# Cross-attention and an FP4 feed-forward on one core: the up half goes by ScalarE and GpSimd, and the sequence is set anew

## The chip, the cores and the metric

The kernel runs on one core of a Trainium2 chip. The metric is the device time of one execution in microseconds. Five engines work side by side, each through its own instructions in order: TensorE (PE; its weight loads are PEld), VectorE (DVE), ScalarE (ACT), GpSimd (POOL) and SyncE (SP), which here issues all DMA transfers. Matmul results lie in PSUM, which GpSimd does not read in this kernel; everything that GpSimd works on is first brought to SBUF by ScalarE.

## The reference

`x` is (16, 512, 256), the context (16, 1601, 192), all float32. One batch element is one "batch" below.

```python
x = x + xattn(layernorm(x), ctx_768)        # 16 heads of 16; softmax(Q K^T / 4) V, then Wo and bias
x = x + ffn(layernorm(x))

def fp4_linear(x, w):                       # blocks of 16 along the last dim, scale = max|x| / 6
    xq = fp4_quant_dequant(x); wq = fp4_quant_dequant(w)
    return jnp.einsum('bsk,nk->bsn', xq, wq)
gate = fp4_linear(x, w_gate)                # 256 -> 704
y = fp4_linear(x, w_up)                     # 256 -> 704
h = jax.nn.silu(gate) * y
return fp4_linear(h, w_down)                # 704 -> 256
```

## The kernel before

**Bodies.** After a prologue ("start") the kernel runs 16 bodies, one a batch ("first", 14 "middle", "last"), and a "tail". A body does the attention of its own batch, the projections of the next batch, and the feed-forward of the batch before; so the feed-forward stands in 15 bodies and once in the tail. 512 query rows are four quarters of 128 rows.

**Steps.** A body has 52 steps: four groups of four heads, 13 key tiles of 128 keys (the last of 65). A step has four score matmuls (128 keys by 512 queries, line 1001), four exponentials on ScalarE (line 1140), and four "weighted" matmuls into `out_ps` (line 1014, fp32). The shift of the softmax is found ahead: for each group ahead of its turn 64 "pieces" (line 1027, 402 keys each) are multiplied, two at a time, and VectorE takes the maximum of each (line 1369). `PIECES_AT` says how many pairs of pieces a step has, `EARLY_PIECES` how many pairs are done in the prologue already.

**The sequence.** `sequence(kind)` writes down one order of all work, and TensorE, ScalarE and VectorE each follow it. Inside a step the order comes from a string of `STEP_ORDERS`: `S01` and `S23` are two scores each, `P` a share of the step's pieces, `V` the weighted matmuls of the oldest step not yet done, and `W` the side events due by half-step 2 x step + 1. Before, there are 13 strings, one for each key tile, used alike by the four groups. Side events ("rounds" where TensorE has work in them) are placed by half-steps: `POST_AT` for the feed-forward of the four quarters, `PRE_AT` and `OWN_AT` for the projections, `TAIL_AT` for the tail. The 17 entries of a quarter are heads_T, out_proj, ln2_stats, ln2_apply, xq_max, xq_scale, xq_T, three gate_up, h_max, h_small, h_scale, h_grid, two h_T, down. GpSimd and SP go by the events alone, in the order of their half-steps. All of these numbers stand in the file by hand; nothing is planned while the kernel runs.

**PSUM.** A ring of seven banks (`RINGS`) serves scores, pieces and rounds in the order of the sequence. `claim` makes TensorE wait until the bank's last user was released: a score by its exponential, a piece by its maximum, a round by whichever engine reads it last (`drained`). VectorE handles a round after the next piece or at the next round.

**A gate_up round.** For 256 hidden columns (the third has 192) TensorE fills one bank with gate (`work[:, 0:w]`) and up (`work[:, w:2w]`), six matmuls (line 964). Then:

```python
act.activation(tanh_g[...], work[:, 0:w], ACT.Tanh, scale=0.5)                       # L1118
dve.scalar_tensor_tensor(out=tanh_g[...], in0=tanh_g[...], scalar=1.0, in1=work[:, 0:w], ...)  # L1323
dve.scalar_tensor_tensor(out=q.h[...], in0=tanh_g[...], scalar=0.5, in1=work[:, w:2*w], ...)   # L1326
```

The last one releases the bank. `tanh_g` has two halves, used in turn; ScalarE waits by `silu_step` for the first product of the round before. Later `h_max`, `h_small` (VectorE), `h_scale` (GpSimd, lines 1428 and 1431) and `h_grid` with the rounding (VectorE lines 1201 and 1203, GpSimd from line 1418) make FP4 of `h`, `h_T` turns it, `down` multiplies it; ScalarE copies that result to `down_out` (line 1107) and GpSimd adds it to `x1` (line 1471). In the tail VectorE instead of GpSimd does the scaling, and the rounding of the quarters in `VECTOR_ROUNDS` (lines 1191 to 1195).

**Keys and queries.** `q_proj` and `k_proj` rounds are copied twice by ScalarE (1083, 1084), GpSimd subtracts to get the low part (1462), and SP's "stack" events then move both parts into `k_stack` and `q_stack`, which pieces and scores read.

Of the kernel before, what the change touches and what calls it, by code (L numbers as in the profile page):

```python
# [31 lines left out]
P = 128  # L32
# [33 lines left out]
]  # L66
TAIL_AT = [
# [7 lines left out]
OWN_AT = [6, 15, 15, 16, 18]  # L75
PRE_AT = [24, 27, 27, 30, 45, 45, 50, 56, 61, 61, 63, 66, 69, 69, 70, 71, 71, 72, 74, 76, 85, 99]
# [3 lines left out]
LN1 = 8  # L80

HEADS_OUT_AT = 3
MAX_AT = [22, 23]
PIECES_AT = [
# [4 lines left out]
]  # L89
EARLY_PIECES = 3  # L90
STEP_ORDERS = ['P S01 W P S23 P V', 'S01 P W P S23 P V', 'S01 P W S23 P V', 'S01 P W P S23 P V', 'S01 P W P S23 P V', 'S01 P W P S23 P V', 'S01 P W P S23 P V', 'S01 P W P S23 P V', 'S01 P W P S23 P V', 'S01 P W S23 P V', 'S01 P W P S23 P V', 'S01 P P S23 W P V', 'S01 P S23 P V']
# [8 lines left out]
VECTOR_ROUNDS = [1, 3]  # L100
# [92 lines left out]
def build(nc, x, ctx_768, Wq, Wk, Wv, Wo, bo, w_gate, w_up, w_down, out):  # L193
# [74 lines left out]
    for step in range(STEPS):  # L268
        ready = step - (STEPS - VALUES_LEFT)
        VALUES_LEFT -= min(STEP_ORDERS[step % KEY_TILES].split().count("V"), ready)  # L270

# [18 lines left out]
    def sequence(kind):  # L290
# [52 lines left out]
        def put_events(until):  # L343
            while pending and pending[0][0] <= until:
                for e in pending.pop(0)[1]:
                    put(0, "event", e)
                    put_rounds([e])

        of, n = 1, 2 * EARLY_PIECES
        for g in range(PHASES):  # L350
            for m in range(KEY_TILES):

                step = g * KEY_TILES + m
                left, slots = 2 * PIECES_AT[g][m], STEP_ORDERS[m].count("P")
                for what in STEP_ORDERS[m].split():
# [38 lines left out]
    def count(batch, per, k):  # L394

        return batch * per + k
# [70 lines left out]
    with ctx:  # L467
# [89 lines left out]
        silu_step = sem("silu_step")  # L557
        inv_ready = sem("inv_ready")
# [108 lines left out]
        def released(kind, batch, item):  # L667

            what, *of = item
            if what == "round":  # L670
                return drained(kind, batch, of[0])
            if what == "scores":
                return probs_ready, count(batch, NSCORES * PHASES, PER_GROUP * of[0] + of[1] + 1)
            return pieces_max, count(batch, NPIECE * PHASES, NPIECE * of[0] + of[1] + 1)

# [370 lines left out]
        def _(act):  # L1046
            def handle(kind, batch, event):
# [121 lines left out]
        def _(dve):  # L1169
# [35 lines left out]
            def handle(kind, batch, event):  # L1205
# [112 lines left out]
                elif name == "gate_up":  # L1318
# [5 lines left out]
                                             op0=ALU.add, op1=ALU.mult).then_inc(silu_step, 1)  # L1324
                    dve.wait_ge(silu_step, count(old, n * QT, n * t + j + 1))
                    dve.scalar_tensor_tensor(out=q.h[:, j * GW:j * GW + w], in0=tanh_g[:, half, 0:w], scalar=0.5,  # L1326
                                             in1=work[:, w:2 * w], op0=ALU.mult, op1=ALU.mult).then_inc(this_drained, 1)
                elif name in ("h_max", "h_small", "h_scale", "h_grid"):
# [3 lines left out]
                    if name == "h_max":  # L1332
                        dve.wait_ge(*drained(kind, batch, ("gate_up", t, len(gate_w) - 1)))
# [68 lines left out]
        def _(pool):  # L1402
# [32 lines left out]
            def handle(kind, batch, event):  # L1435
# [3 lines left out]
                if name in ("ln2_stats", "ln2_apply", "xq_max", "xq_scale", "h_scale", "h_grid"):  # L1439
                    q = quarter(kind, event[1])  # L1440
# [107 lines left out]
```

## Time and profile before

| | |
|---|---|
| Median of 3 runs | 3379.75 us (3379.11 to 3393.36) |
| The profiled execution | 3376.89 us, span 3375.1 us |
| Granted TensorE clock, mean | 0.965 |
| Busy, share of the span | PE 95%, PEld 49%, DVE 80%, ACT 68%, POOL 33% |
| Instructions | 55778 |
| DMA queue share of 16 engines | 27.0% |

The span runs from the first to the last instruction. Busy shares are means over stretches of different kinds: a prologue of 79 us to the first score, the bodies, and a tail of 88 us after the last score. A matmul's end is modelled, so a busy PE may stand still. A wait is put down to the engine whose signal came last.

### The profile page before, as it was taken

The page shows a single profiled execution, that of the slowest core. Times are in us where ns is not written, and L with a number is a line of the kernel's source. Part 1 is how long each engine was busy: PE and PEld are TensorE (multiplying, and loading weights), DVE is VectorE, ACT ScalarE, POOL GpSimd, SP SyncE. Part 2 cuts the span into 40 slices and gives each one's busy share as a digit, 9 for nine tenths or more (in the row PEclk, how much of TensorE's full clock was granted, in tenths as well). Part 3 has the DMA queues.
Part 4 walks back from the last instruction along what each step waited for, and adds up shares of the span by engine and source line. Part 5 has one row for each costly group of instructions (what it writes and reads, how often), then busy time and mean ns, then how long its engine had stood idle before and what let it go on. Part 6 is the DMA issues. An engine that isn't in the chain of part 4 may idle for free.

```text
span 3375.1 us, 55778 instructions
## 1 busy us (share of the span) xinstructions
PE 3209.6 (95%) x19606; PEld 1657.6 (49%) x19606; DVE 2698.0 (80%) x6009; ACT 2282.7 (68%) x4692; POOL 1097.4 (33%) x1411
## 2 busy tenths in 40 slices
PE   6899999999999999999999999999999999999996
PEld 4344544545455454544545455454544545454444
DVE  6877788888887878878887888878878888887855
ACT  2666677676766767767676776767767677766761
POOL 0213333243333333324343333333333333332332
PEclk6998999999999999999999999999999999999987
DMA  3332133232222322133232222322133232222200
GB/s 78 71 54 47 36 60 56 35 65 39 52 48 40 66 45 50 36 59 58 35 65 35 51 53 42 64 45 53 35 58 56 35 66 43 46 48 46 41 14 8
DMA packets 120783, 163.29 MB, mean 48 GB/s; under 512 B 47125, under 2 KB 93606, under 8 KB 120506
## 3 DMA queue, kind: packets, MB, share of 16 engines
q1 hardware_dynamic: 120506, 159.73, 27.0%
q8 instruction: 158, 2.59, 0.3%
q14 instruction: 119, 0.97, 0.1%
HBM read 46.22 MB, written 8.39 MB: 16 GB/s over the span
## 4 chain that ended last, share of the span: by engine, by line
PE 72%; DVE 11%; ACT 4%; SPq 4%; DMA 4%; POOL 2%; issue 2%; POOLq 0%; DVEq 0%; ACTq 0%
PE out_ps L1014 17%; PE ring L1001 14%; PE ring L1027 13%; PE ring L964 8%; DVE piece_max L1369 6%; PE ring L975 5%; PE ring L931 3%; PE ring L939 3%; DMA k_stack<-k_parts 2%; ACT probs L1140 2%; SPq L820 2%; PE ring L920 2%; DMA q_stack<-neg_rows 2%; PE ring L955 2%; PE ring L949 1%
## 5 line engine op out<-in xcount | busy, mean ns | idle before, releaser
L1369 DVE TENSOR_REDUCE piece_max<-ring 128x1 f32<-128x402 f32 x4096 | 2072.4, 567 | 454.3 <-PE ring L1027 443.5
L1140 ACT ACTIVATE probs<-ring 128x512 f32<-128x512 f32 (+1 forms) x3328 | 1774.8, 605 | 560.4 <-PE ring L1001 544.5
L1014 PE MATMUL out_ps<-probs,v_ones 128*17 128x512 f32 x6656 | 898.9, 612 | 0.8 <-ACT probs L1140 0.8
L1001 PE MATMUL ring<-q_stack,k_stack 50*128 50x512 f32 (+1 forms) x3328 | 841.3, 469 | 37.2 <-DMA q_stack<-neg_rows 24.7
L1027 PE MATMUL ring<-k_stack,q_stack 48*128 48x402 f32 x4096 | 818.9, 391 | 44.8 <-DMA k_stack<-k_parts 32.9
L1001 PEld LDWEIGHTS ring<-q_stack,k_stack 50*128 50x128 f32 (+1 forms) x3328 | 349.5, 184 | 815.4 <-issue 262.0
L1027 PEld LDWEIGHTS ring<-k_stack,q_stack 48*128 48x128 f32 x4096 | 448.6, 192 | 307.9 <-DVE piece_max L1369 95.7
L964 PE MATMUL ring<-wgu_T,xq_T 128*128 128x512 f32 (+1 forms) x1080 | 252.5, 382 | 1.9 <-POOL xq_T L1474 0.5
L1418 POOL TENSOR_TENSOR h<-h,h_grid 128x704 f32<-128x704 f32 (+1 forms) x68 | 101.6, 1494 | 460.2 <-DVE h_grid L1203 460.2
L964 PEld LDWEIGHTS ring<-wgu_T,xq_T 128*128 128x128 f32 x1080 | 192.7, 188 | 53.2 <-issue 22.8
L1014 PEld LDWEIGHTS out_ps<-probs,v_ones 128*17 128x17 f32 x6656 | 110.7, 95 | 218.6 <-issue 183.5
L1428 POOL TENSOR_SCALAR h<-h 128x704 f32<-128x704 f32 x60 | 46.7, 778 | 460.4 <-DVE h_small L1180 458.7
L975 PE MATMUL ring<-wd_T,h_T 128*128 128x256 f32 x744 | 175.3, 385 | 1.2 <-ACT h_T L1128 1.2
L1118 ACT ACTIVATE tanh_g<-ring 128x256 f32<-128x256 f32 (+1 forms) x192 | 70.3, 366 | 147.5 <-PE ring L964 146.4
L939 PE MATMUL ring<-wv_sb,ctx_T 128*128 128x256 f32 (+1 forms) x1040 | 166.1, 308 | 2.6 <-DVE wv_sb L1237 1.9
L931 PE MATMUL ring<-ctx_T,wk_sb 128*128 128x512 f32 (+1 forms) x640 | 155.2, 385 | 6.2 <-DVE ctx_T L1247 5.6
L939 PEld LDWEIGHTS ring<-wv_sb,ctx_T 128*128 128x128 f32 (+1 forms) x1040 | 143.1, 203 | 31.4 <-issue 31.4
L975 PEld LDWEIGHTS ring<-wd_T,h_T 128*128 128x128 f32 x744 | 136.3, 190 | 38.5 <-issue 19.9
L1467 POOL TENSOR_TENSOR x<-x,resid 128x256 f32<-128x256 f32 x60 | 44.0, 733 | 293.9 <-ACT x L1103 293.9
L1323 DVE SCALAR_TENSOR_TENSOR tanh_g<-tanh_g,ring 128x256 f32<-128x256 f32 (+1 forms) x192 | 76.1, 396 | 72.3 <-ACT tanh_g L1118 66.7
L931 PEld LDWEIGHTS ring<-ctx_T,wk_sb 128*128 128x128 f32 x640 | 109.4, 191 | 47.3 <-issue 10.7
L1462 POOL TENSOR_TENSOR k_parts<-k_parts 128x512 fp32r<-128x512 f32 (+1 forms) x127 | 113.0, 901 | 55.5 <-ACT k_parts L1084 54.1
(170 smaller groups left out, 2662.6 us busy)
## 6 DMA issues: line engine op xcount, KB each, us to landing
k_stack<-k_parts SPq DMA_DIRECT2D x256, 200.1 KB, 4.7
k_stack<-k_parts SPq DMA_DIRECT2D x256, 100.1 KB, 4.3
ctx_in<-in_ctx SPq DMA_DIRECT2D x47, 384.0 KB, 4.0
q_stack<-q_parts SPq DMA_DIRECT2D x256, 64.0 KB, 2.3
x_in<-in_x SPq DMA_DIRECT2D x16, 512.0 KB, 5.5
q_stack<-q_parts SPq DMA_DIRECT2D x256, 32.0 KB, 2.0
resid<-in_x SPq DMA_DIRECT2D x62, 128.0 KB, 2.7
out<-x SPq DMA_DIRECT2D x62, 128.0 KB, 1.8
```

Source lines behind the costliest of these rows:

```text
L931: last = pe.matmul(work[:, 0:w], wk_sb[:, by, e * P:(e + 1) * P], ctx_T[:, of, a:a + w], start=(n == 0), stop=(n == len(PRODUCTS) - 1))
L939: last = pe.matmul(work[0:r, u * D:(u + 1) * D], ctx_T[:, of, a:a + r], wv_sb[:, by, :], start=(n == 0), stop=(n == len(PRODUCTS) - 1))
L964: last = pe.matmul(work[:, 0:w], quarter(kind, t).xq_T[:, of, k, :], wgu_T[:, k, by, a:a + w], start=(k == n == 0), stop=(k == 1 and n == ...
L975: last = pe.matmul(work[:, 0:D], quarter(kind, event[1]).h_T[:, c, :], wd_T[:, c, :], start=(c == 0), stop=(c == FT - 1))
L1001: pe.matmul(ring[0:r, bank(kind, batch, item), :], k_stack[rows, at, m * P:m * P + r], q_stack[rows, at, :], start=True, stop=True).then_i ...
L1014: last = pe.matmul(out_ps[32 * j:32 * j + V1, :], v_ones[0:r, batch % 2, m, PER_GROUP * g + j, :], probs[0:r, prob_slot(batch, step, j), : ...
L1027: pe.matmul(ring[:, bank(kind, batch, item), 0:PW], q_stack[rows, at, t * P:(t + 1) * P], k_stack[rows, at, a:b], start=True, stop=True).t ...
L1140: act.activation(probs[0:r, prob_slot(batch, step, j), :], ring[0:r, at, :], ACT.Exp, scale=SCORE_SCALE).then_inc(probs_ready, 1)
L1323: dve.scalar_tensor_tensor(out=tanh_g[:, half, 0:w], in0=tanh_g[:, half, 0:w], scalar=1.0, in1=work[:, 0:w], op0=ALU.add, op1=ALU.mult).th ...
L1369: dve.tensor_reduce(piece_max[:, g % 2, 2 * u + half, t, c:c + 1], ring[:, at, 0:PW], AX_X, ALU.max).then_inc(pieces_max, 1)
L1418: pool.tensor_tensor(src, src, grid, ALU.add).then_inc(done, 1)
L1462: pool.tensor_tensor(low.bitcast(F32R), low, parts[:, 0, a:a + w], ALU.subtract).then_inc(split_step, 1)
```

## The change

Outside the tail the up half of a gate_up round is now copied by ScalarE at half scale into `down_out`, ahead of the tanh. VectorE makes only the first product, which releases the bank, and GpSimd multiplies `tanh_g` by `down_out` into `h`, counted by a new semaphore `h_product`. ScalarE waits for the product of the round before, and for the last use of `down_out` by a down projection, before it copies; `down` waits in turn for the products ahead of it. `h_max` waits for GpSimd. In the tail only the placing changes: `TAIL_AT`, and `VECTOR_ROUNDS` is [3] for [1, 3], so quarter 1's rounding is GpSimd's. The order inside a step is looked up in a table of 18 strings for each of 52 steps; `w` in a string releases the events of half-step 2 x step only. All positions and piece counts are set anew.

```diff
 POST_AT = [
-    [5, 9, 12, 13, 14, 16, 19, 21, 22, 22, 22, 26, 30, 31, 39, 39, 40],
-    [20, 22, 22, 24, 32, 36, 40, 43, 48, 48, 48, 48, 49, 52, 60, 62, 65],
-    [54, 57, 57, 58, 58, 60, 64, 66, 66, 66, 67, 67, 68, 74, 80, 80, 97],
-    [65, 67, 68, 75, 79, 81, 85, 86, 86, 86, 88, 91, 96, 96, 100, 101, 103],
+    [4, 8, 11, 11, 14, 16, 19, 20, 20, 21, 22, 25, 27, 28, 39, 39, 40],
+    [20, 21, 25, 29, 38, 39, 40, 42, 47, 48, 48, 50, 50, 54, 62, 62, 64],
+    [44, 46, 57, 60, 61, 63, 64, 68, 68, 68, 69, 73, 73, 75, 80, 80, 97],
+    [66, 67, 68, 72, 78, 81, 85, 87, 87, 89, 90, 94, 95, 96, 100, 101, 103],
 ]
 TAIL_AT = [
-    [0, 2, 2, 2, 2, 2, 5, 5, 5, 7, 7, 7, 7, 9, 13, 13, 15],
-    [0, 4, 4, 4, 5, 6, 7, 8, 8, 9, 9, 11, 11, 12, 19, 21, 23],
-    [0, 4, 7, 7, 8, 9, 16, 16, 17, 17, 17, 19, 20, 20, 23, 26, 26],
-    [9, 9, 9, 12, 13, 14, 18, 19, 19, 19, 20, 23, 23, 23, 26, 26, 33],
+    [2, 3, 3, 3, 4, 6, 9, 12, 12, 12, 12, 14, 14, 14, 16, 19, 19],
+    [2, 3, 5, 5, 7, 8, 11, 14, 15, 15, 15, 17, 17, 17, 22, 22, 24],
+    [3, 5, 7, 8, 8, 12, 14, 15, 16, 16, 18, 18, 20, 20, 24, 24, 25],
+    [6, 7, 8, 11, 14, 14, 16, 20, 20, 20, 22, 23, 24, 24, 27, 28, 35],
 ]
-OWN_AT = [6, 15, 15, 16, 18]
-PRE_AT = [24, 27, 27, 30, 45, 45, 50, 56, 61, 61, 63, 66, 69, 69, 70, 71, 71, 72, 74, 76, 85, 99]
+OWN_AT = [7, 14, 14, 16, 17]
+PRE_AT = [20, 20, 20, 35, 45, 45, 48, 49, 55, 62, 62, 65, 68, 69, 71, 71, 71, 72, 74, 77, 85, 100]
-LN1 = 8
+LN1 = 9
-HEADS_OUT_AT = 3
+HEADS_OUT_AT = 2
 PIECES_AT = [
-    [3, 3, 3, 4, 1, 1, 1, 4, 3, 3, 3, 0, 2],
-    [4, 2, 1, 2, 3, 1, 3, 4, 4, 2, 3, 1, 1],
-    [1, 2, 3, 1, 2, 3, 3, 4, 4, 3, 4, 1, 3],
-    [3, 3, 2, 4, 4, 1, 1, 3, 3, 4, 3, 0, 1],
+    [2, 2, 2, 4, 2, 1, 1, 4, 5, 2, 3, 0, 2],
+    [4, 0, 3, 1, 3, 3, 1, 4, 4, 3, 3, 1, 0],
+    [2, 1, 1, 3, 1, 4, 4, 3, 5, 3, 5, 0, 3],
+    [4, 3, 1, 4, 4, 3, 1, 3, 2, 3, 5, 0, 0],
 ]
-EARLY_PIECES = 3
-STEP_ORDERS = ['P S01 W P S23 P V', 'S01 P W P S23 P V', 'S01 P W S23 P V', ...]
+EARLY_PIECES = 4
+ORDERS = [
+    "P S01 W P S23 P V",
+    "S01 P W P S23 P V",
+    "S01 P W S23 P V",
+    "S01 P P S23 W P V",
+    "S01 P S23 P V",
...
+    "S01 P W P V S23 P",
+    "w S01 P V S23 P W",
+    "S01 w P S23 P W V",
+]
+STEP_ORDERS = [
+    [15, 14, 17, 1, 14, 2, 1, 1, 1, 15, 1, 3, 4],
+    [16, 2, 17, 2, 2, 15, 1, 1, 1, 2, 2, 3, 17],
+    [3, 3, 1, 15, 0, 1, 1, 16, 15, 2, 1, 3, 4],
+    [2, 1, 2, 0, 2, 1, 5, 17, 6, 1, 6, 8, 14],
+]
-VECTOR_ROUNDS = [1, 3]
+VECTOR_ROUNDS = [3]
@@ sequence
-                    elif what == "W":
-                        put_events(2 * step + 1)
+                    elif what in ("w", "W"):
+                        put_events(2 * step + (what == "W"))
@@ scalar
                 elif name == "down":
                     if event[1] or old:
                         act.wait_ge(x1_done, count(old, QT, event[1]))
+                    act.wait_ge(h_product, count(old, len(gate_w) * QT, rounds_ahead(kind, event, "gate_up")))
                     act.copy(down_out[:], work[:, 0:D]).then_inc(this_drained, 1)
@@
-                    if n * t + j >= 2:
-                        act.wait_ge(silu_step, count(old, n * QT, n * t + j))
+                    if kind != "tail":
+                        if n * t + j or old:
+                            act.wait_ge(h_product, count(old, n * QT, n * t + j))
+                        downs = rounds_ahead(kind, event, "down")
+                        if downs or old:
+                            act.wait_ge(x1_done, count(old, QT, downs))
+                        act.activation(down_out[:, 0:w], work[:, w:2 * w], ACT.Copy, scale=0.5)
+                    elif n * t + j >= 2:
+                        act.wait_ge(silu_step, n * t + j)
...
@@ vector
                     dve.scalar_tensor_tensor(out=tanh_g[:, half, 0:w], in0=tanh_g[:, half, 0:w], scalar=1.0, in1=work[:, 0:w],
-                                             op0=ALU.add, op1=ALU.mult).then_inc(silu_step, 1)
-                    dve.wait_ge(silu_step, count(old, n * QT, n * t + j + 1))
+                                             op0=ALU.add, op1=ALU.mult).then_inc(silu_step if kind == "tail" else this_drained, 1)
+                    if kind != "tail":
+                        return
@@ gpsimd
+                elif name == "gate_up" and kind != "tail":
+                    t, j = event[1:]
+                    w, n = gate_w[j], len(gate_w)
+                    pool.wait_ge(*drained(kind, batch, event))
+                    pool.tensor_tensor(q.h[:, j * GW:j * GW + w], tanh_g[:, (n * t + j) % 2, 0:w], down_out[:, 0:w], ALU.mult).then_inc(h_product, 1)
```

`rounds_ahead` is a new helper that counts the rounds of a name ahead of an event.

## Rows read from the trace of the kernel before

**Rows 1.** the page, part 1: engine, busy us (share of the span), instructions
```profile
PE 3209.6 (95%) x19606; PEld 1657.6 (49%) x19606; DVE 2698.0 (80%) x6009; ACT 2282.7 (68%) x4692; POOL 1097.4 (33%) x1411
```

**Rows 2.** busy us of PE, PEld, DVE, ACT, POOL; clock, DMA share, GB/s; steady stretch
```profile
280.00:3111.00 2831.00, 2748.30 (x17122) 1416.69 (x17124) 2314.46 (x5164) 1993.56 (x4102) 962.43 (x1245) 0.98 0.28 49
```

**Rows 3.** who waited for whom, 280 to 3111 us: total us, times, longest
```profile
ACT probs L1140 <- PE ring L1001: 458.5, 727, 3.2
...
PEld ring L1001 <- DVE piece_max L1369: 169.8, 265, 1.7
...
PEld ring L1001 <- ACT probs L1140: 136.9, 233, 1.3
...
PEld ring L1027 <- DVE piece_max L1369: 77.6, 224, 1.7
...
PEld ring L1001 <- ACT k_parts L1084: 47.6, 56, 0.9
...
DVE tanh_g L1323 <- ACT tanh_g L1118: 42.8, 85, 1.0
...
PEld ring L1001 <- DVE h L1326: 39.0, 42, 1.0
...
PEld ring L1027 <- ACT probs L1140: 33.4, 92, 0.9
```

**Rows 4.** groups by line and shape, whole run: busy us, mean ns, idle before
```profile
L1369 DVE TENSOR_REDUCE piece_max<-ring 128x1 f32<-128x402 f32 x4096 | 2072.4, 567 | 454.3 <-PE ring L1027 443.5
...
L1001 PE MATMUL ring<-q_stack,k_stack 50*128 50x512 f32 x3072 | 786.8, 473 | 37.2 <-DMA q_stack<-neg_rows 24.7 <-issue 3.6 <-DVE piece_max L1369 1.9
...
L1431 POOL TENSOR_TENSOR h<-h,h_small 128x704 f32<-128x704 f32 x60 | 83.2, 1387 | 5.0
...
L1326 DVE SCALAR_TENSOR_TENSOR h<-tanh_g,ring 128x256 f32<-128x256 f32 x120 | 50.4, 420 | 4.1
...
L1428 POOL TENSOR_SCALAR h<-h 128x704 f32<-128x704 f32 x60 | 46.7, 778 | 460.4 <-DVE h_small L1180 458.7
...
L1471 POOL TENSOR_TENSOR x<-x,down_out 128x256 f32<-128x256 f32 x60 | 43.9, 732 | 195.6 <-ACT down_out L1107 195.6
...
L1107 ACT COPY down_out<-ring 128x256 f32<-128x256 f32 x60 | 22.3, 372 | 115.9 <-PE ring L975 115.9
...
L1326 DVE SCALAR_TENSOR_TENSOR h<-tanh_g,ring 128x192 f32<-128x192 f32 x60 | 21.2, 353 | 2.1
```

**Rows 5.** instructions in order of time, 1665 to 1678 us: start, length
```profile
1668.24 0.38 ACT L1118 ACTIVATE tanh_g<-ring 128x256 f32<-128x256 f32 x1 [0.92 <-PE ring L964]
1668.66 0.42 DVE L1323 SCALAR_TENSOR_TENSOR tanh_g<-tanh_g,ring 128x256 f32<-128x256 f32 x1 [0.21 <-ACT tanh_g L1118]
...
1669.64 0.38 ACT L1118 ACTIVATE tanh_g<-ring 128x256 f32<-128x256 f32 x1 [1.02 <-PE ring L964]
...
1670.70 0.33 ACT L1118 ACTIVATE tanh_g<-ring 128x192 f32<-128x192 f32 x1 [0.67 <-PE ring L964]
...
1671.31 1.09 ACT L1140 ACTIVATE probs<-ring 128x512 f32<-128x512 f32 x2 [0.28 <-PE ring L1001]
```

**Rows 6.** what TensorE itself waited for, whole run
```profile
PE ring L1027 <- DMA k_stack<-k_parts: 32.9, 16, 3.4
```

**Rows 7.** the tail, 3287.5 to 3375.1 us: engines, then two groups
```profile
3287.50:3375.10 87.60, 55.91 (x212) 41.36 (x208) 47.99 (x108) 14.16 (x37) 22.24 (x27) 0.80 0.02 8
...
L1418 POOL TENSOR_TENSOR v_ones<-v_ones,probs 128x704 f32<-128x704 f32 x2 | 3.0, 1516 | 21.3 <-DVE probs L1203 21.3
...
L1191 DVE TENSOR_TENSOR v_ones<-v_ones,probs 128x704 f32<-128x704 f32 x2 | 1.8, 892 | 0.1
```

**Rows 8.** lengths of single lines: min/median/max ns
```profile
L1369 DVE TENSOR_REDUCE piece_max<-ring x4096: 511/567/579, 35.6 to 3248.9; 128x1 f32<-128x402 f32 x196
...
L1178 DVE TENSOR_SCALAR h_small<-h_small x68: 173/186/733, 93.8 to 3271.7; 128x44 f32<-128x44 f32 x62, 128x32 f32<-128x32 f32 x5, 64x32 f32<-64x32 f32 x1
```

More of the change, by code:

```diff
@@ L79 @@
 STACK0_AT = [18, 70]
-LN1 = 8
-HEADS_OUT_AT = 3
+LN1 = 9
+HEADS_OUT_AT = 2
 MAX_AT = [22, 23]
 PIECES_AT = [
[4 rows of a table removed]
-]
-EARLY_PIECES = 3
-STEP_ORDERS = ['P S01 W P S23 P V', 'S01 P W P S23 P V', 'S01 P W S23 P V', 'S01 P W P S23 P V', 'S01 P W P S23 P V', 'S01 P W P S23 P V', 'S01 P W P S23 P V', 'S01 P W P S23 P V', 'S01 P W P S23 P V', 'S01 P W S23 P V', 'S01 P W P S23 P V', 'S01 P P S23 W P V', 'S01 P S23 P V']
[4 rows of a table added]
+]
+EARLY_PIECES = 4
[5 more added lines that the diff above has]
+    "S01 P S23 P V",
+    "S01 P S23 P W V",
+    "S01 P S23 W V P",
+    "V S01 P W P S23 P",
+    "S01 V P W P S23 P",
+    "V W S01 P S23 P",
+    "S01 P V W S23 P",
+    "W V S01 P S23 P",
+    "S01 W V P S23 P",
+    "S01 P W V S23 P",
+    "P S01 P W S23 V",
+    "S01 P W P V S23 P",
[3 more added lines that the diff above has]
+STEP_ORDERS = [
[4 rows of a table added]
+]
 RINGS, RING_FOR = (7,), (0, 0, 0, 0)
@@ L269, in build @@
         ready = step - (STEPS - VALUES_LEFT)
-        VALUES_LEFT -= min(STEP_ORDERS[step % KEY_TILES].split().count("V"), ready)
+        VALUES_LEFT -= min(ORDERS[STEP_ORDERS[step // KEY_TILES][step % KEY_TILES]].split().count("V"), ready)
     def transposes(event):
@@ L353, in sequence @@
                 step = g * KEY_TILES + m
-                left, slots = 2 * PIECES_AT[g][m], STEP_ORDERS[m].count("P")
-                for what in STEP_ORDERS[m].split():
+                parts = ORDERS[STEP_ORDERS[g][m]].split()
+                left, slots = 2 * PIECES_AT[g][m], parts.count("P")
+                for what in parts:
                     if what == "P":
@@ L557, in build @@
         silu_step = sem("silu_step")
+        h_product = sem("h_product")
         inv_ready = sem("inv_ready")
@@ L674, in released, with rounds_ahead @@
             return pieces_max, count(batch, NPIECE * PHASES, NPIECE * of[0] + of[1] + 1)
+        def rounds_ahead(kind, event, name):
+            return sum(e[0] == name and n < ROUND[kind][event] for e, n in ROUND[kind].items())
         def run(eng, body):
@@ L1115, in handle @@
                     w, n = gate_w[j], len(gate_w)
-                    if n * t + j >= 2:
-                        act.wait_ge(silu_step, count(old, n * QT, n * t + j))
+                    if kind != "tail":
[7 more added lines that the diff above has]
+                        act.wait_ge(silu_step, n * t + j)
+                    else:
+                        act.wait_ge(h_product, count(old, n * QT, 0))
                     act.activation(tanh_g[:, (n * t + j) % 2, 0:w], work[:, 0:w], ACT.Tanh, scale=0.5).then_inc(tanh_ready, 1)
@@ L1323, in handle @@
                     dve.scalar_tensor_tensor(out=tanh_g[:, half, 0:w], in0=tanh_g[:, half, 0:w], scalar=1.0, in1=work[:, 0:w],
-                                             op0=ALU.add, op1=ALU.mult).then_inc(silu_step, 1)
-                    dve.wait_ge(silu_step, count(old, n * QT, n * t + j + 1))
+                                             op0=ALU.add, op1=ALU.mult).then_inc(silu_step if kind == "tail" else this_drained, 1)
+                    if kind != "tail":
+                        return
+                    dve.wait_ge(silu_step, n * t + j + 1)
                     dve.scalar_tensor_tensor(out=q.h[:, j * GW:j * GW + w], in0=tanh_g[:, half, 0:w], scalar=0.5,
@@ L1332, in handle @@
                     if name == "h_max":
-                        dve.wait_ge(*drained(kind, batch, ("gate_up", t, len(gate_w) - 1)))
+                        if kind == "tail":
+                            dve.wait_ge(*drained(kind, batch, ("gate_up", t, len(gate_w) - 1)))
+                        else:
+                            dve.wait_ge(h_product, count(old, len(gate_w) * QT, len(gate_w) * (t + 1)))
                         fp4_max(src, q.h_small, h_step)
@@ L1438, in handle @@
                 name = event[0]
-                if name in ("ln2_stats", "ln2_apply", "xq_max", "xq_scale", "h_scale", "h_grid"):
+                if name in ("ln2_stats", "ln2_apply", "xq_max", "xq_scale", "gate_up", "h_scale", "h_grid"):
                     q = quarter(kind, event[1])
```

## Prediction

> **What bounds the kernel now.** I read the busy shares first, then the steady stretch, then who waited for whom there, and only then single instructions. The shares put TensorE at 95% [rows 1], which looks like a bound. It is not a clean one: 3072 score matmuls of 0.473 us would take 1453 us one after the other and cover 786.8 [rows 4], so they run side by side in pairs, and a span covers waiting too. From 280 to 3111 us, fourteen bodies of 202.2 us each, VectorE is busy 2314.46 of 2831 us (81.8%), ScalarE 1993.56 (70.4%), GpSimd 962.43 (34.0%) [rows 2]. All matmul work is in one in-order sequence that takes its PSUM banks in turn from a ring of seven, so a late release by VectorE or ScalarE stops everything behind it. The waits of the weight loads show whose releases are late: VectorE's 169.8 + 77.6 + 39.0 = 286.4 us, ScalarE's 136.9 + 33.4 + 47.6 = 217.9 us [rows 3]. The 39.0 us are the release of gate/up banks by line 1326, the very instruction that the change removes. So the bound is a ring served by two engines, VectorE the more loaded, and neither saturated over a whole batch. VectorE's own work is 4096 reductions of 0.567 us [rows 4], which the change leaves alone.
>
> **The change part by part.** It acts on the 12 gate/up rounds of a body, in 15 bodies: 180 rounds (120 of 256 columns, 60 of 192). The tail's 12 keep both VectorE instructions.
>
> (a) VectorE loses the second product, 50.4 + 21.2 = 71.6 us [rows 4]. What of it counts? The first product now starts later, because ScalarE's copy of the up half stands ahead of the tanh. Before, VectorE sat waiting for a tanh 85 times in the steady stretch [rows 3] (14 of the 15 bodies, so about 90 times in 15). There the copy's time, 0.372 us for 128x256 from PSUM (line 1107 has this shape) [rows 4], is handed back as waiting: 90 x 0.372 = 33 us. Net relief 71.6 - 33 = 38 us. If every gate wait were lengthened, 180 x 0.372 = 67 us would go back and 5 us be left; if VectorE always came late, 71.6 us stay. I take 38 as relief and let three quarters of it reach the end, since VectorE is the more loaded server but not the only one: -28 us (bounds 0 and -72).
>
> (b) ScalarE gains 180 copies: 120 x 0.372 + 60 x about 0.32 (an estimate: the narrow tanh is 0.05 us shorter [rows 5]) = 64 us, and reaches about 72.6% of the steady stretch. I cost this at nothing beyond (a), because ScalarE sat before exponentials for 458.5 us in 727 pieces, 0.63 us each [rows 3]: one 0.37 us copy is caught up by the next pair. If that cover is gone it is +64 us.
>
> (c) GpSimd gains 180 products. Line 1471 is the same shape from SBUF, 0.732 us [rows 4]; 120 x 0.732 + 60 x about 0.55 = 121 us, at 34% busy. Its time alone is nothing. The wait that comes with it is not: there is one `down_out` buffer, so the copy of round n waits until GpSimd has finished round n-1. Behind that copy on ScalarE stand its own tanh (and VectorE's release of the bank) and all following exponentials. Where rounds follow each other on TensorE, they come 1.40 us apart (tanh at 1668.24, then 1669.64), and the third, whose operands are narrower, 1.06 us after the second [rows 5]. The new loop is copy 0.37 + tanh 0.38 + first product 0.42 + GpSimd's 0.73 + three handoffs of 0.04 to 0.1 (the rows show 0.04 from tanh to VectorE) = 2.1 us. So an adjacent round costs ScalarE 0.7 us, an adjacent third 1.05 us. How many are adjacent? By the tables, with "W" releasing the events of both halves of a step: quarter 0 has two rounds at half-step 20 and the third behind four other rounds; quarter 1 has 42, 47, 48, three different steps; quarter 2 has all three at 68; quarter 3 has two at 87 and one at 89. That is three waits of 0.7 and one of 1.05 per body, 3.15 us, 47 us in all. The triple of quarter 2 is followed by the q and k rounds of the next batch, so its exponentials would have been late anyway, and elsewhere the 0.63 us gaps absorb much. I put a third on the path: +15 us (bounds 0 and +47). The old wait, for the first product alone, closed within 0.84 us and never bound.
>
> (d) What stands behind GpSimd's products in its queue: in quarter 2 the q and k splits (line 1462), for which SP's stack transfers wait. TensorE already waited 32.9 us for k_stack, 16 times, 2.1 us each [rows 6]. The last k round stays at half-step 71 and h_scale (0.78 + 1.39 us of GpSimd [rows 4]) moves from 68, ahead of the splits, to 73, behind them; three products take 2.0 us of its place. I count nothing (bounds -15 and +15, one us a body).
>
> (e) The new orders and positions. Before, 6 of 12 gate rounds were adjacent to their predecessor, now 4, and pieces are moved by ones and twos (one more before the first body). No instruction is added. This can only move the 504 us of bank waits (286.4 + 217.9) [rows 3]. A tenth either way is my bound, -50 and +50; spreading VectorE's gate bursts and giving each of 52 steps its own order lets releases come nearer to their claims, so I take -18 us, 1.2 us a body, the least certain term.
>
> (f) The tail, 87.6 us with TensorE busy for 55.91 [rows 7]. Quarter 1's rounding goes from VectorE (three of 0.89 us, line 1191 for one [rows 7]) to GpSimd (three of about 1.5 us, line 1418 for one [rows 7]), +1.8 us in that quarter; but three quarters' chains no longer stand in VectorE's strict order with it, and gate rounds come after all out_proj rounds, so statistics run earlier. I take -4 us (bounds -12 and +6).
>
> Sum against the profiled execution, 3376.89 us (span 3375.1 plus 1.8): -28 + 0 + 15 + 0 - 18 - 4 = -35, so 3342. The median of the three runs is 2.9 us above that execution: 3345 us.
>
> One rule of the Trainium skill speaks against (a) and (c). The trace shows the piece reduction at 511/567/579 ns and the 44-element scaling of line 1178 at 173/186/733 ns [rows 8]: the reduction is never held up, the scaling sometimes for half a us. The Trainium skill (Perfetto Trace Analysis, Optimizing Scalar/DVE Operations) warns that VectorE and GpSimd share an SBUF read port, so that offloading between these two might not help; by that rule the rows of line 1178 are such meetings, and those of the reduction show none. If GpSimd's extra 4% of the time held up as many more of the some 400 instructions on lines 1178, 1201 and 1203 by half a us each, that were 400 x 0.04 x 0.5 = 8 us, and the sum would be 3353 instead of 3345.
>
> **Rivals.**
> Slower: the down_out loop binds. The mechanism is (c) with its full price: ScalarE stands 3.15 us per body, the exponentials behind it release their banks late, the ring of seven fills, and VectorE waits for the same tanhs so that its relief shrinks to the 5 us end of (a). For it: in the triple of rows 5 the exponential came 0.28 us after the last tanh, no slack there. Against it: only one of four quarters keeps a triple. +47 (the loop) - 5 (what is left of (a)) - 4 (the tail) = +38, 3418; with a quarter of the copies of (b) uncovered (+16) the far end is 3434, and with (e) paying half (-9) it is 3409: I take 3410. It decides from the point where more than about two thirds of the 47 us reaches the path.
> No change: the ring's waits are only renamed. VectorE's 286 us go over to ScalarE as ScalarE's load rises; (a) pays 5 to 10 us, (c) costs as much, the orders pay nothing: 3376 to 3384, about 3380.
> Much faster: VectorE truly bounds. Steps where it was busy for all of the time pay the whole 71.6 us less the 33, and (e) reaches its bound: -38 - 50 - 8 (the tail) = -96, so 3284; half-way from the forecast to there it is 3314.
> That the change doesn't do what it says: the removed product could leave VectorE's busy time while the wait for tanh takes all its place; that is the 5 us end of (a) and falls under "no change".
>
> **How the numbers follow.** Forecast case 0.52 (3320 to 3368, around 3345), much faster 0.12, no change 0.20, slower by the loop 0.16. About 0.5%, 17 us, is what a measurement here can tell from none. Below 3363 lie nine tenths of the forecast case and all of the much faster one, with a sliver of the third: 0.60. Above 3397 lies the slower case but a little: 0.16. The rest, 0.24, is within. The range for 8 in 10 goes from well into the much faster case to the near half of the slower one: 3293 to 3402 us.
>
> **What would show it.** VectorE's busy time down by 72 us (2698 to about 2626) and ScalarE's up by 64, GpSimd's by 121: that is certain, and says nothing of time. (a) is right if VectorE's waits before the first product grow by some 33 us and no more than 67, and the weight loads' waits for VectorE fall from 286 us by more than those for ScalarE rise. (c) shows as idle time of ScalarE before its new copies ended by GpSimd: below 50 us in total it was sized right, above 80 us the slower rival is at work. (d) shows in TensorE's wait for k_stack, 2.1 us a body now. (e) is right if the body's period falls from 202.2 to about 200.1 us, and wrong if it stays while (a) shows. (f) is the stretch after the last score. A period above 203 us makes the prediction wrong as a whole.

## The result and the profile after

The changed kernel takes 3446.64 us (median of 4 runs, 3442.68 to 3460.54) against 3379.43 us, a ratio of 1.0197 with a 95% interval of 1.0157 to 1.0236: 2% slower, where 1% faster was forecast, and 45 us above the end of the range. The profiled execution took 3444.58 us; its span is 3442.8 us, 67.7 us more than before.

Part 1 of the page of the changed kernel answers to [rows 1]:

```profile
PE 3255.2 (95%) x19606; PEld 1694.3 (49%) x19606; DVE 2599.6 (76%) x5826; ACT 2324.4 (68%) x4872; POOL 1224.4 (36%) x1594
```

VectorE's busy time fell by 98 us (72 of it the second products), ScalarE's rose by 42 (a tanh starts 0.28 us after its copy of 0.38, so the spans overlap), GpSimd's by 127. The work went where it was sent; the time did not follow. Where the span went shows from the first score of each body. The bodies are counted here up to the first score of the last step, and the tail from there. Before, the sixteen bodies took from 79.2 to 3287.2 us and the tail 87.9; now 79.4 to 3367.8 and 75.0. The bodies cost 80.4 us more, the tail gave 12.9 back. Body 0, which has no feed-forward at all and so nothing of the split, went from 201.0 to 207.8 us.

The groups that answer to [rows 4], by line and shape, in the changed kernel:

```profile
L1546 POOL TENSOR_TENSOR h<-tanh_g,down_out 128x256 f32<-128x256 f32 x120 | 88.2, 735 | 301.0 <-DVE tanh_g L1364 301.0
...
L1154 ACT ACTIVATE down_out<-ring 128x256 f32<-128x256 f32 x120 | 46.1, 384 | 116.7 <-PE ring L995 96.5 <-PE ring L983 18.9 <-PE ring L936 1.4
...
L1546 POOL TENSOR_TENSOR h<-tanh_g,down_out 128x192 f32<-128x192 f32 x60 | 35.8, 596 | 117.9 <-DVE tanh_g L1364 117.9
...
L1154 ACT ACTIVATE down_out<-ring 128x192 f32<-128x192 f32 x60 | 21.3, 356 | 30.1 <-issue 21.2 <-PE ring L995 8.9
```

Every new instruction costs what was put down for it (0.384 against 0.372 us, 0.735 against 0.732). The loop is there too. In quarter 2 of body 8, in order of time (start, length; in brackets idle time and what ended it):

```profile
1868.30 0.38 ACT L1154 ACTIVATE down_out<-ring 128x256 f32<-128x256 f32 x1 [0.89 <-PE ring L995]
1868.58 0.38 ACT L1159 ACTIVATE tanh_g<-ring 128x256 f32<-128x256 f32 x1
1868.99 0.42 DVE L1364 SCALAR_TENSOR_TENSOR tanh_g<-tanh_g,ring 128x256 f32<-128x256 f32 x1 [0.46 <-ACT tanh_g L1159]
1869.49 0.74 POOL L1546 TENSOR_TENSOR h<-tanh_g,down_out 128x256 f32<-128x256 f32 x1 [2.41 <-DVE tanh_g L1364]
1870.31 0.39 ACT L1154 ACTIVATE down_out<-ring 128x256 f32<-128x256 f32 x1 [1.36 <-PE ring L995]
...
1872.31 0.33 ACT L1154 ACTIVATE down_out<-ring 128x192 f32<-128x192 f32 x1 [1.34 <-issue]
```

Copy follows copy after 2.01 and 2.00 us (2.1 was put down), against 1.40 and 1.06 between the tanhs of [rows 5]. The wait is put down to TensorE or to "issue"; what ScalarE really waited for is GpSimd, whose product ends at 1870.23 (1869.49 + 0.74), 0.08 us before the copy. Over the whole run 61 copies began within 0.13 us of the end of such a product, and 4 adjacent rounds in each of 15 bodies had been counted. So the loop costs about 3 us of ScalarE a body as said, 47 us in all. That cannot be 80 us.

What had not been looked for shows in the waits of the steady stretch, 280 to 3111 us, which answer to [rows 3]:

```profile
PEld ring L1032 <- DVE piece_max L1415: 174.5, 286, 1.7
...
PEld ring L1032 <- ACT probs L1181: 139.9, 232, 0.9
...
DVE tanh_g L1364 <- ACT tanh_g L1159: 103.7, 97, 1.6
...
PEld ring L1032 <- DMA q_stack<-neg_rows: 88.0, 48, 3.5
PEld ring L1058 <- DVE piece_max L1415: 72.1, 159, 0.9
...
PE ring L1032 <- DMA q_stack<-neg_rows: 44.7, 29, 2.5
...
PEld ring L1032 <- DVE tanh_g L1364: 35.4, 40, 1.0
...
PEld ring L1032 <- ACT k_parts L1115: 26.9, 41, 0.9
PEld ring L1058 <- ACT probs L1181: 26.4, 88, 0.5
```

The waits for banks are much as before (174.5 and 139.9 for 169.8 and 136.9); the six rows of bank waits add up to 475 us, where [rows 3] gave 504 (the stretch now holds 13.7 bodies for 14). What grew is the wait for `neg_rows`, the shift rows. In the kernel before it was:

```profile
PEld ring L1001 <- DMA q_stack<-neg_rows: 30.4, 29, 2.0
...
PE ring L1001 <- DMA q_stack<-neg_rows: 21.7, 29, 1.7
```

The first scores of a group of heads wait for their shift rows. These rows take a long way: maxima of all pieces of the group (VectorE), a transpose (TensorE), a cast (ScalarE, line 1126), four transfers (SP). Step 12 to 13 of body 8, changed kernel:

```profile
1781.81 0.25 ACT L1126 CAST neg_rows<-ring 32x128 fp32r<-32x128 f32 x1
...
1782.08 2.65 SPq L851 DMA_DIRECT2D q_stack<-neg_rows  x4
...
1783.41 1.05 PE L1045 MATMUL out_ps<-probs,v_ones 128*17 128x512 f32 x8
...
1785.88 0.50 PE L1032 MATMUL ring<-q_stack,k_stack 50*128 50x512 f32 x2 [1.42 <-DMA q_stack<-neg_rows]
```

and the same place in the kernel before:

```profile
1742.17 0.25 ACT L1095 CAST neg_rows<-ring 32x128 fp32r<-32x128 f32 x1
...
1742.45 2.66 SPq L820 DMA_DIRECT2D q_stack<-neg_rows  x4
...
1745.38 0.64 PE L1027 MATMUL ring<-k_stack,q_stack 48*128 48x402 f32 x4
...
1746.26 0.50 PE L1001 MATMUL ring<-q_stack,k_stack 50*128 50x512 f32 x2 [0.24 <-DMA q_stack<-neg_rows]
```

From cast to scores it is 4.1 us in both. Before, four pieces filled the last of it, because a group's first step had the order `P S01 ...`. The new table has `w S01 P ...` (entry 16) for step 13 and `S01 P ...` for steps 0, 26 and 39: the scores stand first and TensorE stands still for 1.42 us. Such an idle time of TensorE ahead of a step's first score is called a gap below.

### The profile page after: what moved, and what is told of

Same layout as the page of the kernel before. It is cut to its first block and busy times, and to the rows that moved or that the text cites. A ratio compares the mean times of both kernels' runs of the same rounds, so it can differ in the third digit from the quotient of the medians.

```text
span 3442.8 us, 55990 instructions
## 1 busy us (share of the span) xinstructions
PE 3255.2 (95%) x19606; PEld 1694.3 (49%) x19606; DVE 2599.6 (76%) x5826; ACT 2324.4 (68%) x4872; POOL 1224.4 (36%) x1594
## 5 line engine op out<-in xcount | busy, mean ns | idle before, releaser
L1045 PE MATMUL out_ps<-probs,v_ones 128*17 128x512 f32 x6656 | 919.9, 626 | 1.9 <-ACT probs L1181 1.9
L1058 PE MATMUL ring<-k_stack,q_stack 48*128 48x402 f32 x4096 | 791.3, 390 | 49.6 <-DMA k_stack<-k_parts 29.0
L1058 PEld LDWEIGHTS ring<-k_stack,q_stack 48*128 48x128 f32 x4096 | 459.8, 195 | 291.6 <-DVE piece_max L1415 95.6
L1546 POOL TENSOR_TENSOR h<-tanh_g,down_out 128x256 f32<-128x256 f32 x180 | 124.0, 689 | 418.9 <-DVE tanh_g L1364 418.9
L995 PE MATMUL ring<-wgu_T,xq_T 128*128 128x512 f32 (+1 forms) x1080 | 262.8, 388 | 0.6 <-POOL xq_T L1520 0.4
L1154 ACT ACTIVATE down_out<-ring 128x256 f32<-128x256 f32 x180 | 67.5, 375 | 146.8 <-PE ring L995 105.4
L1508 POOL TENSOR_TENSOR q_parts<-q_parts 128x512 fp32r<-128x512 f32 x31 | 39.6, 1278 | 273.4 <-ACT q_parts L1115 273.4
```

Of the source, the lines that this page charges most:

```text
L995: last = pe.matmul(work[:, 0:w], quarter(kind, t).xq_T[:, of, k, :], wgu_T[:, k, by, a:a + w], start=(k == n == 0), stop=(k == 1 and n == ...
L1045: last = pe.matmul(out_ps[32 * j:32 * j + V1, :], v_ones[0:r, batch % 2, m, PER_GROUP * g + j, :], probs[0:r, prob_slot(batch, step, j), : ...
L1058: pe.matmul(ring[:, bank(kind, batch, item), 0:PW], q_stack[rows, at, t * P:(t + 1) * P], k_stack[rows, at, a:b], start=True, stop=True).t ...
L1508: pool.tensor_tensor(low.bitcast(F32R), low, parts[:, 0, a:a + w], ALU.subtract).then_inc(split_step, 1)
L1546: pool.tensor_tensor(q.h[:, j * GW:j * GW + w], tanh_g[:, (n * t + j) % 2, 0:w], down_out[:, 0:w], ALU.mult).then_inc(h_product, 1)
```

## The clock: what a gap costs beyond its length

The granted clock has two levels in these traces, 1.2 and 2.4 GHz. At 1.2 GHz the kernel before spent 241 us (31 stretches), the changed one 349 us (42 stretches). Steps 26 to 28 of two bodies of the kernel before, the same work with the same gap ahead of it (columns: busy us of PE, PEld, DVE, ACT, POOL, then clock, DMA share and GB/s):

```profile
780.30:790.20 9.90, 9.66 (x66) 4.31 (x66) 7.31 (x16) 8.42 (x17) 5.86 (x5) 1.00 0.60 90
979.60:991.90 12.30, 12.30 (x66) 5.54 (x66) 7.40 (x16) 8.50 (x17) 5.81 (x5) 0.72 0.48 72
```

The same 66 matmuls take 9.9 us at full clock and 12.3 us where the clock fell to 1.2 GHz, 2.3 us after the end of the gap. VectorE, ScalarE and GpSimd did the same work in both. Step 27 alone is 3.59 or 5.43 us. Among bodies 1 to 14 it was the long one in 7 before, and it took 5.0 us or more in all 14 of the split-only kernel below (e1), whose gap there is 1.86 us in place of 1.16 in the mean. So a stall before a group's first scores can be paid twice, once as a gap and once, in some bodies, as slow TensorE after it. The length of the gap does not decide it alone: e13 below has the gap of e12 and keeps the clock. At a mean clock of 0.72 the second row holds 6.9 us at 1.2 GHz (12.3 x 0.28 x 2) and lost 2.4 us, 0.35 us for each. At that rate the 108 us more of the changed kernel are some 38 us. The Trainium skill (TensorE: Matmul & The Clock Gate, Terms) puts the penalty at about half of the throttled time, which would be 54 us here, an estimate. The rows give less. That VectorE and ScalarE set part of the pace would explain it, but no run shows it.

## The experiments

Each kernel is compared with the kernel before on the same chip; "before" was 3378 to 3382 us in all four sets. Steps are read from the start of each step's first score, median over bodies 1 to 14; "time at 1.2 GHz" is that of the whole profiled execution.

**The two halves of the change, and the tail.** First theory: the placing (tables and orders) costs the time. Rival: the loop of the split costs it.

The split with every table of before (e1):

```diff
-POST_AT, PRE_AT, OWN_AT, LN1, HEADS_OUT_AT, PIECES_AT, EARLY_PIECES, STEP_ORDERS, TAIL_AT, VECTOR_ROUNDS of the changed kernel
+those of the kernel before (the split's code stays)
```

> The split of the gate product over ScalarE and GpSimd, with every position, piece count and step order of before. Theory P (the placing costs the time: big bursts of rounds at step 10 and step 34, TensorE waiting for the shift rows before step 13, TensorE at half clock more often): about 3380, between 3360 and 3400, body period 201 to 203 us. Theory L (the loop copy, tanh, first product, GpSimd's product costs it): six adjacent rounds a body at 0.6 to 1.0 us, so 3430 or more, period above 205 us.

3500.41 us, ratio 1.0372 (1.0334 to 1.0409), as theory L had it, and worse than the whole change. The steps that grew are few: 12 (+0.65), 25 (+1.17), 26 (+1.85), 27 (+0.91), 33 (+0.30), 34 (+2.39), 38 (+0.33), 43 (+0.89). Steps 10, 11, 21, 22 and 39 shrank by 0.1 to 0.25 us each, 23 and 28 grew by as much, and the other 37 are equal to 0.02 us. Steps 24 to 26 of body 8:

```profile
1837.43 2.02 DVE L1410 TENSOR_REDUCE piece_max<-ring 128x1 f32<-128x402 f32 x4
...
1840.58 0.38 ACT L1154 ACTIVATE tanh_g<-ring 128x256 f32<-128x256 f32 x1
1840.99 0.42 DVE L1359 SCALAR_TENSOR_TENSOR tanh_g<-tanh_g,ring 128x256 f32<-128x256 f32 x1 [0.86 <-ACT tanh_g L1154]
...
1841.49 0.73 POOL L1541 TENSOR_TENSOR h<-tanh_g,down_out 128x256 f32<-128x256 f32 x1 [10.13 <-DVE tanh_g L1359]
1842.31 0.33 ACT L1149 ACTIVATE down_out<-ring 128x192 f32<-128x192 f32 x1 [1.35 <-PE ring L970]
...
1842.74 0.24 ACT L1121 CAST neg_rows<-ring 32x128 fp32r<-32x128 f32 x1
...
1843.95 0.89 DVE L1208 TENSOR_REDUCE h_small<-h 128x44 f32<-128x704 f32 x1 [0.71 <-POOL h L1541]
...
1846.86 0.80 PE L1027 MATMUL ring<-q_stack,k_stack 50*128 50x512 f32 x2 [1.76 <-DMA q_stack<-neg_rows]
```

The cast of the shift rows (line 1121) stands behind the waiting copy on ScalarE. It comes 5.31 us after the start of VectorE's reductions at 1837.43; before it came 4.14 us after the same point:

```profile
1783.95 2.01 DVE L1369 TENSOR_REDUCE piece_max<-ring 128x1 f32<-128x402 f32 x4
...
1788.09 0.24 ACT L1095 CAST neg_rows<-ring 32x128 fp32r<-32x128 f32 x1
...
1792.20 0.51 PE L1001 MATMUL ring<-q_stack,k_stack 50*128 50x512 f32 x2 [1.13 <-DMA q_stack<-neg_rows]
```

The 1.17 us go through SP to the scores, the gap grows from 1.13 to 1.76 us, and the scores' span is 0.80 us in place of 0.51, at the low clock. The loop's price is not idle ScalarE but what waits behind ScalarE.

The placing with both products on VectorE (e2):

```diff
-act.activation(down_out[:, 0:w], work[:, w:2 * w], ACT.Copy, scale=0.5)   # and GpSimd's product, and their waits
+dve.scalar_tensor_tensor(out=q.h[...], in0=tanh_g[...], scalar=0.5, in1=work[:, w:2 * w], ...)   # as before
```

> The changed kernel's positions, piece counts and orders, with both products on VectorE as before. Theory P: as slow as the changed kernel, 3430 to 3470, the tail about 75 us. Theory L: about 3368, the time of before less the 13 us of the tail.

3425.55 us, ratio 1.015 (1.0103 to 1.0197). The bodies take 3269.6 us against 3208.0 (+61.6), the tail 73.6. The time lies between the two expectations. Both theories hold in part: the placing costs without the split, and the split costs without the placing.

The tail alone (e3):

```diff
 # kernel before
+TAIL_AT, VECTOR_ROUNDS = those of the changed kernel
```

> The kernel before with the changed TAIL_AT and VECTOR_ROUNDS alone. Both theories: the stretch after the last score goes from 88 to about 75 us and nothing else moves, 3380 - 13 = 3367. If the shorter tail came from the changed bodies, it stays at 88 us and the time at 3380.

3367.99 us, ratio 0.9974 (0.9956 to 0.9992), the tail 75.1 us. As expected.

**The loop by itself (e4, e6).** The up half is copied straight into `h`, where GpSimd multiplies in place; a copy then waits only for the product two rounds back. The waits that kept the copies and the down projections from each other's use of `down_out` go as well.

```diff
-act.wait_ge(h_product, count(old, n * QT, n * t + j))
-act.activation(down_out[:, 0:w], work[:, w:2 * w], ACT.Copy, scale=0.5)
+act.wait_ge(h_product, count(old, n * QT, n * t + j - 1))
+act.activation(quarter(kind, t).h[:, j * GW:j * GW + w], work[:, w:2 * w], ACT.Copy, scale=0.5)
...                                                          # GpSimd reads h in place of down_out
```

In the changed kernel (e4):

> The changed kernel with the up half copied straight into h (GpSimd multiplies in place), so that a copy waits only for the product two rounds back and down_out is free. Theory L: the four adjacent waits a body go, 3 us a body, 3400 or less. Theory P: 3435 to 3447, the period falls from 206.7 us by less than 0.7 us.

3420.62 us, ratio 1.0128 (1.0088 to 1.0169): 26 us less than the changed kernel. Neither expectation fits; the loop, with the other waits for the one buffer, is worth 26 us there.

With the placing of before (e6):

> Positions and orders of before, product split over ScalarE and GpSimd, but the up half copied straight into h, so no round waits for the one before. Theory L (of the 122 us of the split alone, the wait for the single down_out buffer is the larger part): 3380 to 3410. Rival C (the copy's own time ahead of the tanh and the later h_max cost it): 3450 to 3500. If VectorE was the bound: below 3363.

3407.68 us, ratio 1.0065 (1.0043 to 1.0087), at the upper end of theory L. Of the 122 us of the split alone, 93 are the loop, with its six adjacent rounds a body.

**The orders of a group's first step (e5).** The edit also moves the side events and the weighted matmuls of these four steps, since whole strings are changed.

```diff
-    [15, 14, ...], [16, 2, ...], [3, 3, ...], [2, 1, ...]
+    [0, 14, ...], [0, 2, ...], [0, 3, ...], [0, 1, ...]      # 0 is "P S01 W P S23 P V"
```

> The changed kernel with the order 'P S01 W P S23 P V' in the first step of each group (steps 0, 13, 26, 39), so that pieces stand ahead of the first scores there as before. Theory G (the new orders put the first scores of a group ahead of all pieces, TensorE waits 1.4 to 1.7 us for the shift rows and its clock drops after): the two gaps shrink to about 0.3 and 1.2 us, the half-clock time falls from 349 us towards 250, and the time to 3415 to 3430. Rival R (only the two bursts at steps 10 and 34 cost): 3440 to 3450.

3417.74 us, ratio 1.0103 (1.0054 to 1.0152): 29 us less than the changed kernel, from four entries of the table. The mean gaps before steps 13 and 26 went from 1.44 and 1.65 to 0.87 and 1.26 us, the time at 1.2 GHz from 349 to 308 us. Body 0, which has no feed-forward, went from 207.8 back to 200.6 us. The time is as theory G had it, though the first gap did not shrink to 0.3 us, and the clock not by that gap: in steps 13 to 16 the time at 1.2 GHz even rose, from 7.3 to 9.0 us a body, while it fell from 2.9 to 0.7 in steps 26 to 28 and from 3.2 to 1.5 in steps 38 to 40.

**Which half of the placing.**

```diff
 # e7: kernel before
+PIECES_AT, EARLY_PIECES, STEP_ORDERS of the changed kernel
 # e8: kernel before
+POST_AT, PRE_AT, OWN_AT, LN1, HEADS_OUT_AT of the changed kernel
```

> Both products on VectorE, positions of the events as before; only the piece counts, EARLY_PIECES and the step orders are the changed kernel's. Theory G: the orders carry most of the placing's loss in the bodies (60 us): 3410 to 3440. Rival E (the event positions carry it): 3370 to 3395.

> Both products on VectorE, piece counts and orders as before; only POST_AT, PRE_AT, OWN_AT, LN1 and HEADS_OUT_AT are the changed kernel's. Theory G: 3380 to 3400. Rival E: 3420 to 3450, with long steps 10 and 34.

3632.47 us (1.0745) and 3541.81 us (1.0461). Both expectations were wrong by far: either half alone is much worse than both together. The tables are fitted to each other, and asking which half carries the loss has no answer. In e7 step 31 grew by 4.0 and step 32 by 5.7 us, while step 33 shrank by 5.3.

**Single loads.** VectorE's relief with nothing in its place (e10; the second product is left out in the bodies, and a one-column memset releases the bank):

```diff
+                    if kind != "tail":
+                        dve.memset(pause[:], 0.0).then_inc(this_drained, 1)
+                        return
```

> The kernel before with VectorE's second product left out in the bodies (h keeps old contents; a memset of one column releases the bank instead), nothing put in its place. It measures the relief of VectorE alone, 180 x (0.40 - 0.06) = 61 us of its work. As predicted, three quarters of the relief count: 3330 to 3340. If VectorE's load was not the bound in those steps: 3363 to 3378.

3369.08 us, ratio 0.9958 (0.9939 to 0.9977): 12 us by the medians, 14 by the ratio, for 53 us less of VectorE's busy time (2644.8 for 2698.0). That is the second expectation, not the one that the prediction implied.

ScalarE's copy with nothing taken away (e11):

```diff
+                    if kind != "tail":
+                        act.activation(quarter(kind, t).h[...], work[:, w:2 * w], ACT.Copy, scale=0.5)
                     act.activation(tanh_g[...], work[:, 0:w], ACT.Tanh, scale=0.5)
```

> The kernel before with ScalarE's copy of the up half added ahead of the tanh (into h, where VectorE's second product then writes), both products still on VectorE. It measures the 64 us of ScalarE alone. If its gaps before the exponentials hide them, as predicted: 3375 to 3390. If the later bank release and the shift rows behind the copies count: 3400 to 3440.

3417.35 us, ratio 1.0108 (1.009 to 1.0127): 36 us, for 46 us more of ScalarE's busy time. That is the second expectation: the copies are not hidden. Only steps 25 (+0.36), 34 (+0.38), 43 (+0.26) and 44 (-0.21) changed in a fixed way, 0.8 us a body or 12 us; steps 26 to 28, 38 and 39 changed with the gap ahead of step 26 (1.57 us in the mean for 1.16) and the clock, and the time at 1.2 GHz rose from 241 to 337 us.

**Repairs and the best version.** Both repairs (pieces first, up half in `h`) in the changed kernel (e12):

> The changed kernel with both repairs: pieces ahead of the first scores of each group, and the up half copied straight into h. If loop and orders are separate causes, their gains add: 3446 - 29 - 26 = 3391, between 3380 and 3402. If both only give the same clock loss back: 3408 to 3420.

3391.72 us, ratio 1.0034 (1.0021 to 1.0047). The gains add, 29 and 26 us to 55, well within the scatter of the runs: two separate causes.

On top of it, the rounds that made step 10 long moved back (e13):

```diff
-PRE_AT = [20, 20, 20, 35, ...
+PRE_AT = [24, 27, 27, 35, ...
```

> The kernel with both repairs (pieces first, up half straight into h; 3392 us), with the two x_T rounds and the first ctx_T round moved from half-step 20, where they stand between gate rounds in the 8.7 us step 10, back to 24, 27 and 27 as in the kernel before. Theory S (the burst at step 10 is what is left of the placing's loss, 24 us in the bodies): 3370 to 3385. Rival D (the work only moves, and piles up in steps 12 and 13 beside the wait for the shift rows): 3390 to 3410.

3368.28 us, ratio 0.9963 (0.9949 to 0.9977): 23 us less, 2 us below the range of theory S. But the burst's own length is not what was won: step 10 shrank by 1.30 us, and step 13, which got the rounds, grew by 1.35, as rival D had it. What is left are steps 14 and 15, 1.8 us shorter together. Step 14 of body 5, in e12 and in e13:

```profile
1147.10:1151.50 4.40, 4.35 (x20) 1.45 (x16) 2.87 (x7) 2.76 (x5) 3.21 (x5) 0.50 0.88 120
1146.70:1149.60 2.90, 2.54 (x22) 0.94 (x18) 2.55 (x7) 2.59 (x6) 2.17 (x2) 1.00 0.87 130
```

In e12 the clock was at 1.2 GHz for part of steps 14 and 15 in 10 of the 14 bodies, in e13 in none. Step 14 took 2.83 us in the four bodies of e12 in which it ran at full clock, and 2.83 or 2.84 us in all of e13. The gap ahead of step 13 is 0.66 us in the one and 0.67 in the other. So the gain came through the clock; why it held in e13 no run shows. With three repairs the changed kernel is 10 us faster than the kernel before, about what the new tail alone gives.

The split only for quarters 0 and 3, which have nothing urgent behind their copies in the old placing; once there, with the new tail (e9), and once on e12 (e14):

```diff
+        SHARED_QUARTERS = (0, 3)
-                elif name == "gate_up" and kind != "tail":
+                elif name == "gate_up" and shared(kind, event[1]):      # likewise on ScalarE and VectorE
```

> Positions and orders of before in the bodies; the split with the up half copied straight into h only for quarters 0 and 3, where the split without the loop shortened steps 10, 11 and 44 by 0.1 to 0.4 us and nothing stands behind the copies that a transfer waits for; quarters 1 and 2 on VectorE; the tail of the changed kernel. If the losses of the split sit in quarter 1 (the shift rows) and quarter 2 (the q and k splits on GpSimd): 3367 - 0.75 us x 15 = 3352 to 3362, faster than both kernels. If they sit in the copy itself wherever it stands: 3370 to 3385.

> The kernel with both repairs, and the split only for quarters 0 and 3, quarters 1 and 2 on VectorE. If the rule found on the old placing (no copy ahead of the shift rows, no product ahead of the q and k splits) holds for the new one: 3380 to 3388. If the new positions of quarters 1 and 2 already avoid it: 3390 to 3398.

The first took 3354.22 us, ratio 0.9919 (0.9903 to 0.9936), as its first expectation had it, and faster than both kernels; its engines' row is

```profile
PE 3187.4 (95%) x19606; PEld 1649.8 (49%) x19606; DVE 2657.6 (80%) x5916; ACT 2302.8 (69%) x4782; POOL 1162.2 (35%) x1504
```

Of the 27 us, 11 to 13 are the tail's (e3: 10.6 us by the medians, 12.8 in the profile), the other 14 to 16 the split of six rounds a body. The second took 3405.93 us, ratio 1.0075 (1.0054 to 1.0096), 14 us worse than e12, against both expectations: at its new positions quarter 1 has one gate round before the shift rows, and VectorE's second product lengthened steps 21, 22 and 24 by 0.11, 0.34 and 0.42 us. Step 25 gave 0.25 of it back, and the time at 1.2 GHz rose from 301 to 337 us. Which quarters should be split depends on the placing.

## Why the prediction was wrong, point by point

The failed step is (e), the new orders and positions. It was taken as -18 us, bounded at 50 us either way, as a tenth of the 504 us of bank waits. The placing alone cost 3425.6 - 3378.6 = 47 us, 60 in the bodies with the tail's gain of 13 taken out. Two reasonings in it were wrong. "This can only move the 504 us of bank waits" left out waits for transfers and the clock. The bank waits did fall, to 475 us, and the time rose all the same. The runs show 29 us for the pieces that no longer stood ahead of the first scores (e5) and 23 us for the three rounds moved into step 10, these by way of the clock in steps 14 and 15 (e13; both in the presence of the split). And a bound taken as a share of a total is none: e7, which adds no instruction either, cost 251 us. What would have warned was the 24.7 us that the scores already waited for `neg_rows` [rows 4], read together with the group's first step: the diff showed index 0 of the old strings, `P S01 ...`, give way to strings that begin with `S01` or `w S01`.

(a) The mechanism was right and the size too large. -28 us was taken (0 to -72); with nothing in its place and no copy ahead the relief is worth 12 us (e10). VectorE's wait for the tanh rose from 42.8 to 103.7 us in the steady stretch; the 61 us are within the 33 to 67 that were named, but near the end at which 5 us of relief are left. TensorE's waits for the banks of gate rounds stayed (39.0 before, 35.4 now, by line 1364). VectorE's share of 81.8% was an average. Probably the gate rounds stand in steps where TensorE itself is busy with long rounds and VectorE waits for it, so that its relief falls where it is not needed; no run tests this.

(b) The copies were costed at nothing, the bound at +64; measured +36 (e11). The prediction named tanh and exponentials only. Three more things stand behind a copy on ScalarE: the cast of the shift rows, the q and k copies, the release of the gate bank. That these lacked the cover is read from where the fixed growth of e11 lies (steps 25, 34 and 43) and was not measured one by one.

(c) The loop: length 2.0 us for 2.1, price +26 us here (e4) for +15, within its bounds. On the old placing, with six adjacent rounds, it is 93 us. The prediction's count of four adjacent rounds and its statement that quarter 1 has none hold, and the new positions are better for the split: it costs 122 us on the old tables and 21 on the new ones (3446.6 - 3425.6). The sign that was named for (c) was no test. ScalarE stood 82.0 us ahead of the 61 copies that GpSimd released, over the mark of 80, but much of that it had stood before too: 0.92 and 1.02 us ahead of the tanhs of [rows 5], for TensorE.

(d) as said: TensorE's own wait for k_stack was 29.0 us in the whole run, 32.9 before [rows 6].

(f) -13 us for -4, just outside the bounds: the gate rounds after all out_proj rounds and quarter 1 on GpSimd together took 12.9 us off the tail.

The terms as measured: placing +60, tail -13, loop +26, copy and relief together -5 (3420.6 - 3425.6), sum +68 for the 67 measured. These are differences between runs in a chain, so the sum had to come out; the -5 is within the scatter. On the old placing the relief is -12 and the copy +36, and both together without the loop +26 (e6), so there the split could only lose. The slower rival was right in sign and wrong in kind: its loop is 26 of the 67 us. The 8 us that were set beside the sentence on the shared read port did not come: the 408 instructions on lines 1178, 1201 and 1203 took 131.1 us before and 125.5 us now, and the piece reduction has the same mean, 568 ns for 567.

What stays open: some 8 us of the placing's 60 that no single run carries, what makes the clock fall in one kernel and hold in another behind the same gap, and how far the clock's share and the gaps' can be told apart; no run held the clock fixed.

## What to carry to other kernels

When work moves to an engine that runs in order, list everything that stands behind it there, down to the quarter-microsecond casts whose result goes through a transfer, and cost each by who waits at its end; the engine's idle share says nothing of this. Where a stage must wait for a transfer, look in the order for what fills the wait, since four entries of a table were worth 29 us here. Hand-set tables that depend on each other can only be judged together, so a re-placing without a run deserves a wide, even range.

## What the runs showed that was not expected

The schedule of the kernel before repeats closely: 43 of the 52 steps keep their length to 0.05 us over fourteen bodies. The others are steps 0 to 2, 25 to 28, 38 and 39. Step 27 has two lengths, 3.59 or 5.43 us, by the granted clock, with gaps of 1.1 us ahead of both. And 46 us more of ScalarE's busy time cost 36 us, of which 12 show as fixed lengths of steps; the rest came with 96 us more at 1.2 GHz. And three rounds moved by two or three steps won 23 us with the same gap behind them; it shows where the clock then held, in steps 14 and 15.
